# Local attention: the keys' sums of squares moved behind the shift on VectorE, inverse lengths made for queries and keys apart

## The reference, cut to what matters

```python
q, k, v = split(x @ Wqkv)                 # per head
q = q / max(norm(q), 1e-12) * q_scale     # norm over the 64 numbers of a head
k = k / max(norm(k), 1e-12) * k_scale
q = q * cos * scale + rotate_half(q) * sin * scale
k = k * cos / scale + rotate_half(k) * sin / scale
sim = 8 * q @ k.T                         # in windows of 32, each with the one before it
out = softmax(mask(sim)) @ v
x = x + out @ Wo
```

## Time and profile before

| | us |
|---|---|
| median of 3 runs | 5129.18 (5128.84 to 5138.17) |
| the profiled execution, its own time | 5126.68 |
| its span, first to last instruction | 5124.9 |
| busy in the span: PE / DVE / ACT / POOL | 4668.2 / 3785.3 / 2776.0 / 2074.7 |
| six layers with local attention | from about 1827 to 5111 us of the span |

### The profile page before, as it was taken

The page is one execution under the profiler, slowest core; times in us unless marked ns, Lnnn a source line. Parts: engine busy times, 40 slices in busy tenths (PEclk is TensorE's granted clock), DMA queues, the critical chain, the costliest instruction groups (busy, mean ns, idle before and its releaser), DMA issues. The chain is left out here.

```text
span 5124.9 us, 167765 instructions
## 1 busy us (share of the span) xinstructions
PE 4668.2 (91%) x74640; PEld 2826.5 (55%) x74640; DVE 3785.3 (74%) x4462; ACT 2776.0 (54%) x3791; POOL 2074.7 (40%) x1499
## 2 busy tenths in 40 slices
PE   7858987998789869999999999999999999999998
PEld 5623334444333346665666466655666566746664
DVE  5667883333778568886888588868887688868885
ACT  4527774223467645555555455555555455555554
POOL 4330000001000046654666366636665466546661
PEclk9979998999799989999999999999999999999999
DMA  0021111000111121111111111111111111111110
GB/s 23 12 69 32 44 43 34 1 0 27 59 38 43 28 62 40 40 37 45 40 40 40 43 40 40 39 40 40 40 40 52 31 40 40 36 43 40 40 40 26
DMA packets 95777, 192.82 MB, mean 38 GB/s; under 512 B 27088, under 2 KB 45520, under 8 KB 93264
## 3 DMA queue, kind: packets, MB, share of 16 engines
q1 hardware_dynamic: 95056, 182.09, 13.9%
HBM read 60.36 MB, written 15.73 MB: 15 GB/s over the span
## 5 line engine op out<-in xcount | busy, mean ns | idle before, releaser
L1846 POOL TENSOR_TENSOR part_of_layer<-part_of_layer,sine_of_layer 128x512 f32<-128x512 f32 x768 | 963.1, 1275 | 640.0 <-DVE sine_of_layer L1718 640.0
L1853 POOL TENSOR_TENSOR part_of_layer<-part_of_layer,inverse_of_layer 128x1024 f32<-128x1024 f32 x384 | 730.3, 1902 | 325.0 <-ACT inverse_of_layer L1601 310.0
L967 ACT ACTIVATE prob_of_ca<-ps 128x1024 f32<-128x1024 f32 (+3 forms) x768 | 594.0, 814 | 263.5 <-PE ps L841 197.6
L1715 DVE TENSOR_TENSOR part_of_layer<-ps,rope 128x1024 f32<-128x1024 f32 x384 | 467.6, 1218 | 46.8 <-ACT square_of_layer L1589 36.0
L1632 ACT ACTIVATE values_of_layer<-ps 128x1024 f32<-128x1024 f32 x192 | 196.5, 1024 | 516.3 <-PE ps L1488 516.3
L1718 DVE TENSOR_TENSOR sine_of_layer<-ps,rope 128x1024 f32<-128x1024 f32 x384 | 465.1, 1211 | 0.0
L859 PE MATMUL ps<-keys_of_ca,queries_of_ca 64*128 64x512 bf16 (+3 forms) x1536 | 331.1, 342 | 133.7 <-DVE top_of_ca L999 60.9
L1507 PEld LDWEIGHTS ps<-prob_t_of_layer,mixed_of_layer 64*64 64x64 f32 x12288 | 338.0, 134 | 161.0 <-issue 151.7
L1416 PE MATMUL ps<-qkv,shifted 128*128 128x512 f32 x768 | 384.3, 622 | 26.8 <-POOL values_of_layer L1856 20.4
L1758 DVE TENSOR_REDUCE total_of_layer<-prob_of_layer 128x16 f32<-128x1024 f32 x192 | 234.2, 1220 | 229.1 <-ACT prob_of_layer L1625 229.1
L1507 PE MATMUL ps<-prob_t_of_layer,mixed_of_layer 64*64 64x32 f32 x12288 | 385.6, 220 | 10.6 <-ACT prob_t_of_layer L1616 6.7
(11 more groups left out here) (206 smaller groups left out, 9248.5 us busy)
## 6 DMA issues: line engine op xcount, KB each, us to landing
mixed_of_layer<-values_of_layer SPq DMA_DIRECT2D x636, 128.0 KB
mixed_of_layer<-values_of_layer SPq DMA_DIRECT2D x264, 64.0 KB
queries_of_ca<-q_parts SPq DMA_DIRECT2D x384, 32.0 KB
keys_of_ca<-k_parts SPq DMA_DIRECT2D x384, 32.0 KB
qkv<-in_qkv SPq DMA_DIRECT2D x6, 1536.0 KB, 6.5
q_parts<-parts_of_ci SPq DMA_DIRECT2D x16, 384.0 KB, 2.6
k_parts<-parts_of_ci SPq DMA_DIRECT2D x16, 384.0 KB, 2.6
rope<-in_rope SPq DMA_DIRECT2D x6, 1024.0 KB, 9.0
```

The source lines that it names most:

```text
L967: nc.scalar.activation(prob[:, i % 2, 2 * two:2 * two + 2, j:], ps[:, 2 * two:2 * two + 2, j:], ACT.Exp, scale=scale).then_inc(raised, 1)
L1715: nc.vector.tensor_tensor(part[:, t % 2, side], by_head(slot), table(2 * side, t), ALU.mult).then_inc(parts, 1)
L1846: nc.gpsimd.tensor_tensor(out, out, sine[:, side, :, (1 - to) * half:(2 - to) * half], ALU.add).then_inc(rotated, 1)
L1853: nc.gpsimd.tensor_tensor(part[:, t % 2, side], part[:, t % 2, side], by, ALU.mult).then_inc(scaled, 1)
```

## The change

The guard and the inversion are split by side, and the keys' half is moved back on two engines.

- DVE: `lengths` and `guard` become `lengths_q` (sum, then guard, 128x16) and `lengths_k` (the same for the keys). `lengths_q` stays behind `rotate_q`. `lengths_k` now stands behind `shift(n-1)`, in front of `add(n-3)` and `totals(n-1)`.
- ACT: `invert` becomes `invert_q`, in its old place, and `invert_k`, behind `raise_p(n-1)` and in front of `out_o(n-2)`. Each is a logarithm and an exponential of 128x16 in place of 128x32.
- POOL: `scale` of a side waits for that side's inverse alone.
- One more guard on DVE, and one more logarithm and exponential on ACT, in every tile.

```diff
-                def invert(t):
+                def invert(t, side, guarded, logged, inverted):
+                    at = slice(side * HEADS, (side + 1) * HEADS)
                     reach(act, l, guarded, t + 1)
-                    nc.scalar.activation(root[:, t % 2], length[:, t % 2], ACT.Ln).then_inc(logged, 1)
+                    nc.scalar.activation(root[:, t % 2, at], length[:, t % 2, at], ACT.Ln).then_inc(logged, 1)
                     reach(act, l, logged, t + 1)
-                    nc.scalar.activation(inverse[:, t % 2], root[:, t % 2], ACT.Exp, scale=-0.5).then_inc(inverted, 1)
+                    nc.scalar.activation(inverse[:, t % 2, at], root[:, t % 2, at], ACT.Exp, scale=-0.5).then_inc(inverted, 1)
...
-                    steps((square_next_q, 0), (square_k, 0), (out_q, 1), (out_k, 1), (out_p, 2), (last(first_invert), 2), (invert, 0),
-                          (out_v, 0), (raise_p, 1), (last(lambda: square_of(0)), 1), (out_o, 2), (shift_low, 4))
+                    steps((square_next_q, 0), (square_k, 0), (out_q, 1), (out_k, 1), (out_p, 2), (last(first_invert), 2), (invert_q, 0),
+                          (out_v, 0), (raise_p, 1), (last(lambda: square_of(0)), 1), (invert_k, 0), (out_o, 2), (shift_low, 4))
...
-                def lengths(t):
-                    reach(dve, l, q_squared, t + 1)
-                    nc.vector.reduce_sum(length[:, t % 2, 0:HEADS], square[:, 0], AX_X).then_inc(summed, 1)
-                    reach(dve, l, k_squared, t + 1)
-                    nc.vector.reduce_sum(length[:, t % 2, HEADS:], square[:, 1], AX_X).then_inc(summed, 1)
+                def lengths(t, side, squared, guarded):
+                    mine = length[:, t % 2, side * HEADS:(side + 1) * HEADS]
+                    reach(dve, l, squared, t + 1)
+                    nc.vector.reduce_sum(mine, square[:, side], AX_X).then_inc(summed, 1)
+                    reach(dve, l, summed, 2 * t + side + 1)
+                    nc.vector.tensor_scalar(mine, mine, LEAST_SQUARE, None, ALU.max).then_inc(guarded, 1)
...
-                def guard(t):
-                    reach(dve, l, summed, 2 * t + 2)
-                    nc.vector.tensor_scalar(length[:, t % 2], length[:, t % 2], LEAST_SQUARE, None, ALU.max).then_inc(guarded, 1)
...
-                    steps((rotate_q, 0), (lengths, 0), (guard, 0), (rotate_k, 0), (maxima, 1), (shift, 1), (last(first_centre), 1),
+                    steps((rotate_q, 0), (lengths_q, 0), (rotate_k, 0), (maxima, 1), (shift, 1), (last(first_centre), 1), (lengths_k, 0),
                           (add, 3), (totals, 1), (even, 1), (last(second_centre), 1), (last(third_centre), 2))
...
-                    reach(pool, l, inverted, t + 1)
+                    reach(pool, l, q_inverted if side == 0 else k_inverted, t + 1)
```

More of the change, by code:

```diff
@@ L1300, in layers @@
         p_turned, weighed, projected = st.sem("p_turned"), st.sem("weighed"), st.sem("projected")
-        q_squared, k_squared, logged = st.sem("q_squared"), st.sem("k_squared"), st.sem("logged")
+        q_squared, k_squared, q_logged, k_logged = (st.sem(n) for n in ("q_squared", "k_squared", "q_logged", "k_logged"))
         q_out, k_out, raised = st.sem("q_out"), st.sem("k_out"), st.sem("raised")
@@ L1304, in layers @@
         q_parts, k_parts, summed = st.sem("q_parts"), st.sem("k_parts"), st.sem("summed")
-        guarded, inverted, topped = st.sem("guarded"), st.sem("inverted"), st.sem("topped")
+        q_guarded, k_guarded, topped = st.sem("q_guarded"), st.sem("k_guarded"), st.sem("topped")
+        q_inverted, k_inverted = st.sem("q_inverted"), st.sem("k_inverted")
         shifted, totalled, evened = st.sem("shifted"), st.sem("totalled"), st.sem("evened")
@@ L1342, in layers @@
                 (k_turned, NT), (scored, NT), (p_turned, NT), (weighed, NT), (projected, NT), (q_squared, NT), (k_squared, NT),
-                (logged, NT), (q_out, NT), (k_out, NT), (raised, NT), (p_out, NT), (o_out, NT), (v_out, NT), (q_parts, 2 * NT),
-                (k_parts, 2 * NT), (summed, 2 * NT), (guarded, NT), (inverted, NT), (topped, NT), (shifted, NT), (totalled, NT),
+                (q_logged, NT), (k_logged, NT), (q_out, NT), (k_out, NT), (raised, NT), (p_out, NT), (o_out, NT), (v_out, NT), (q_parts, 2 * NT),
+                (k_parts, 2 * NT), (summed, 2 * NT), (q_guarded, NT), (k_guarded, NT), (q_inverted, NT),
+                (k_inverted, NT), (topped, NT), (shifted, NT), (totalled, NT),
                 (evened, NT), (over, NT), (added, NT), (q_rotated, 2 * NT), (k_rotated, 2 * NT), (q_scaled, NT), (k_scaled, NT),
@@ L1595, in square_k, with invert_q, invert_k @@
                     nc.scalar.activation(square[:, 1], by_head(KEY_SLOT), ACT.Square).then_inc(k_squared, 1)
-                def invert(t):
+                def invert(t, side, guarded, logged, inverted):
+                    at = slice(side * HEADS, (side + 1) * HEADS)
                     reach(act, l, guarded, t + 1)
-                    nc.scalar.activation(root[:, t % 2], length[:, t % 2], ACT.Ln).then_inc(logged, 1)
+                    nc.scalar.activation(root[:, t % 2, at], length[:, t % 2, at], ACT.Ln).then_inc(logged, 1)
                     reach(act, l, logged, t + 1)
-                    nc.scalar.activation(inverse[:, t % 2], root[:, t % 2], ACT.Exp, scale=-0.5).then_inc(inverted, 1)
+                    nc.scalar.activation(inverse[:, t % 2, at], root[:, t % 2, at], ACT.Exp, scale=-0.5).then_inc(inverted, 1)
+                def invert_q(t):
+                    invert(t, 0, q_guarded, q_logged, q_inverted)
+                def invert_k(t):
+                    invert(t, 1, k_guarded, k_logged, k_inverted)
                 def out_q(t):
@@ L1730, in rotate_k, with lengths_q, lengths_k @@
                     rotate(t, 1, KEY_SLOT, k_squared, k_turned, k_rotated, k_parts)
-                def lengths(t):
-                    reach(dve, l, q_squared, t + 1)
-                    nc.vector.reduce_sum(length[:, t % 2, 0:HEADS], square[:, 0], AX_X).then_inc(summed, 1)
-                    reach(dve, l, k_squared, t + 1)
-                    nc.vector.reduce_sum(length[:, t % 2, HEADS:], square[:, 1], AX_X).then_inc(summed, 1)
+                def lengths(t, side, squared, guarded):
[4 more added lines that the diff above has]
+                    nc.vector.tensor_scalar(mine, mine, LEAST_SQUARE, None, ALU.max).then_inc(guarded, 1)
+                def lengths_q(t):
+                    lengths(t, 0, q_squared, q_guarded)
+                def lengths_k(t):
+                    lengths(t, 1, k_squared, k_guarded)
                 def maxima(t):
```

## The result

The median of the changed kernel is 5138.70 us (20 runs), that of the kernel before, on the same chip, 5131.09 (20 runs): ratio 1.0017 [1.0010, 1.0023] over all runs, which is 8.7 us slower with an interval of 5 to 12 (the two medians are 7.6 apart). The forecast was 6 us slower. The profiled execution of after has a span of 5136.8, that of before 5124.9: 11.9 more.

What follows compares the result with a forecast made beforehand. PE was taken to set the pace in the middle of layers. Middle 0, starts +4.2 and tails +2.0 gave 6 us on 5129.2, so 5135 us, 0.12% slower, with a range of 5127 to 5156.

Steps and rivals of the forecast that it cites:

- PE sets the pace, and the middle costs nothing: Middle of layers: PE busy 13.92 of 14.16 us per tile, so later deliveries within its margins cost zero.
- The late rotation: Middle tiles, DVE: the next rotation starts at 3016.80 in place of 3016.26, 0.54 us later.
- The margin itself: Middle tiles: `turn_k` has 0.62 us to spare behind the rotation's sine product, 0.08 left after the change.
- `even` is held for the whole overlap: DVE's `even` waits until POOL's scaling is done, an overlap of 0.85 us, and lasts near 1.9.
- The start, +4.2: A layer's second tile: held `even` ends 0.7 us later and PE with it; six layers, +4.2 us.
- The tail, +2.0: A layer's end: `project(29)` waits for `out_o`, which comes 0.35 us later; six times, about +2.0 us.
- Faster: Layer starts: shorter pauses keep PE's granted clock at its upper level, near -14 us, 5115; chance 0.08.
- The rotation misses its margin: Middle tiles: a guard of 0.34 makes the chain 0.09 to 0.1 us late per tile, 5152 us; chance 0.28.
- Nothing comes through: Layer edges: `even` not held for the whole 0.85, or early key rotation pays; 5129 to 5131 us; chance 0.14.
- The rival's own counter: Layer starts, argument against the faster case: `turn_k(0)` is not released earlier, so the longest pause stays.

Runs made afterwards that it cites:

- e1: Changed kernel, but a layer's first two tiles keep the old places of the keys' sum, guard and inversion, still split by side; 5119.17 us, 0.9985 of the kernel before.
- e3: Kernel before with guard and inversion split by side, both sides in the old places in all tiles; 5122.27 us, 0.9987 of the kernel before.
- e5: Changed kernel with the keys' inversion one step later on ACT, behind `out_o`; 5243.29 us, 1.0216 of the kernel before.
- e6: e5 with the softmax's reciprocals in PSUM, as in e2; 5132.34 us, 1.0004 of the kernel before.
- e2: Changed kernel with the reciprocals that `even` multiplies by in PSUM, except in a layer's last tile; 5128.34 us, 1.0000 of the kernel before.
- e7: Changed kernel with the new places only in a layer's first two tiles, the other 30 in old places with the split; 5141.78 us, 1.0022 of the kernel before.
- e9: Changed kernel with 30 unused products per layer in PE's pauses in the first two tiles; 5120.90 us, 0.9985 of the kernel before.
- e12: Kernel before with 31 unused products per layer in PE's pauses in the first two tiles; 5111.64 us, 0.9966 of the kernel before.
- e10: e3 with 20 unused products per layer in PE's pauses, none in front of `turn_k(0)`; 5113.86 us, 0.9971 of the kernel before.

## Why the prediction was right, point by point

**PE sets the pace, and the middle costs nothing.** Right. The late rotation was forecast at +0.54 and measured at +0.54, `out_o` at +0.35 and +0.33, the scaling at 4.5 behind the maxima and 4.46, the guard at 0.17 and 0.17, `even` at "near 1.9" and 1.98. The sine product's lead shrank by 0.51 and stayed above the least. The margin itself was 0.54 and not 0.62: what waits is the first weight load of `turn_k` (0.654 behind the sine product, 0.116 at the least), and the prediction read it from the first product. In the tile behind the one shown, `make_k`'s first weight load does wait for `out_o` now, 0.36, but its product keeps its place, 1.82 behind the first of `make_q`, as before. e1 against e3 shows that tiles 2 to 31 lose nothing; e5 and e6 show the price beyond the margin.

**`even` is held for the whole overlap.** Right. The Trainium skill, SBUF — State Buffer, section "Who interferes with whom", says that of two such instructions whichever is issued first keeps the shared ports for its whole duration, and that a VectorE instruction with one SBUF input is free of it. Both halves agree with this case: 2.93 or 2.96 for the later one in e5, 1.22 in e2 with the operand in PSUM.

**The start, +4.2.** Its mechanism is right and its size nearly: `turn_k(0)` gained nothing (12.15 against 12.08), `turn_k(1)` was 0.66 later against 0.7, and with the clock out of the way the six starts differ by 3.6. e2 shows that the hold of `even` is its cause.

**The tail, +2.0.** Right against the split, and not borne out against the kernel before. From the thirtieth to the last maxima the six layers take 153.9 after, and 151.8 and 152.0 in e3 and e7, which have the old places there: 1.9 to 2.1. But the kernel before takes 153.6, and of the filled pair e9 takes 153.8 and e12 152.7. So against it the tail cost 0.3 and 1.1.

The terms give 3.6 and 0.3 to 1.9, that is 4 to 5.5, against 8.7 measured with an interval of 5 to 12.

**What was missing: the granted clock in the starts.** I treated the clock as a chance of a gain (the rival "Faster") and gave the forecast itself no term for it. In the two profiled executions it went the other way: 55.7 us at the lower level after, 37.8 before, and filling the pauses takes 7.9 us more from the starts of after than from those of before. The clocks on record for every run show that this is not a matter of two profiles. The mean granted clock is 0.9647 over the 20 runs of after and 0.9645 over the 11 of e7, which has the same starts. The kernel before has 0.9660, 0.9660 and 0.9663 over 33, 27 and 20 runs on the three chips of the experiments (e7's is the second); e3 has 0.9682 and e1 0.9680. The traces show two levels, full and half, so a mean of c over a span of s is 2 (1 - c) s at the lower one: 363 us for after, 365 for e7, 346 to 349 for before, 326 and 328 for e3 and e1, each known to some 3. So a run of after spends some 15 us more at the lower clock than one of before. The profiled execution of before, at 0.968, was a favourable one, which fits that the two profiles lie 11.9 apart and the runs 8.7.

What these 15 cost is my estimate from the filled kernels: e9 spends 50 us less there than after and is 0.32% faster, e12 41 less than before and 0.34% faster, which is 0.3 to 0.4 us for each. That makes 5 to 7 us, and with the 4 to 5.5 above some 9 to 12, the upper part of the measured interval. It stays an estimate: the two filled kernels still differ by 0.19%, some 9 us, where the terms without the clock account for 4 to 5.5, and the interval of that difference is some 8 us wide either way. That the forecast came as near as it did is in part luck: it had no term for the clock, and of its 2.0 for the tail little is seen against the kernel before. It also called 0.2% too little to be told apart; with 20 runs of each kernel 0.17% was clear of zero.

Set against the split alone, the clock is seen better. By ratio e3 is 0.30% faster than after, 15 us; with the pauses of both filled (e10, e9) 0.14%, 7 us. The gain of e3 over before is not seen once both are filled (e10 is 2 us above e12). Each of these ratios is known to some 0.1%, so the medians point that way and don't prove it; the profiles agree, with 13.7 us at the lower clock in e3 and 37.8 and 55.7 in before and after. By both, the split alone leaves less time at the lower clock, and moving the keys' half in the first two tiles brings it back and adds to it. The prediction looked at the two edits as one and never asked what the split does by itself.

**The rivals.** *The rotation misses its margin*: not seen. The guard took 0.17, not 0.34, and 0.03 was left where I had 0.08. *Nothing comes through*: refuted for the starts by e7, which alone loses 0.22%. *Faster*: the clock did not stay up. The rival's own counter was right that `turn_k(0)` is not released earlier, and understated it: with `make_k(1)` 1.24 earlier the longest pause did not stay but grew, from 2.54 to 3.20. A gain by the clock did come with the split alone, where `turn_k(0)` is hardly earlier either (12.03 against 12.08), and the kernel is 0.13% faster.

## What to carry to other kernels

Where one engine sets the pace without a pause, as in the middle here, moving steps on the others can only cost: work out the margin of each thing that engine waits for, and expect zero as long as every margin holds. Filling a hole in one queue lengthens the chain behind it: here a hole of 1.20 us on DVE was filled, the inverse came 0.7 later, and with it an instruction on POOL that holds DVE. An earlier step on a waiting engine need not shorten its waits: here 2.54 and 1.89 us of pause became 1.30 and 3.20. Cost a loop's first rounds apart, where there is no cover; when an edit has two halves, cost each alone, since here the split alone gained 0.13%, and the move on top of it lost 0.30%.

## What the runs showed of the hardware that I had not expected

- Pauses of PE cost more than their length. In a layer's start four pauses of 1.3 to 3.2 us within some 25 us are followed by 3.4 and 6.8 us at the lower clock. 30 or 31 unused products per layer kept it at 1.00 there and made the kernel 0.32 to 0.34% faster, 16 to 18 us.
- When DVE's `even` and POOL's scaling start within 0.05 us of each other, the one that starts first runs in its own time, and the other takes 2.93 or 2.96 in place of 1.22 or 1.90. In POOL's record too the time that it is held counts as part of the instruction's duration, so a longer POOL instruction need not mean more work.
